# Two placements in an eight-core transformer layer: the softmax broadcasts one tile later, the last output block staggered

## The reference

```python
xn = layernorm(x)
q, k, v = split(xn @ w_qkv + b_qkv)            # 16 heads of 64
attn = softmax(q @ k.T * 64 ** -0.5)           # per head, 2048 x 2048
x = x + (attn @ v) @ w_proj + b_proj
h = fixed(layernorm(x) @ w1 + b1)              # 4096 wide, rounded to 1/256
h = fixed(piecewise_linear_gelu(h))
x = x + fixed(h @ w2 + b2)
```

## Time and profile before

| | us |
|---|---|
| median of 2 runs | 4026.95 (4025.5 to 4028.41) |
| profiled execution, slowest core 2 | 3910.7 span, 3912.19 device time |
| its two attention stages | 828.0 and 804.8 |
| ScalarE busy | 2506.1 (64%) |
| TensorE busy (matmuls) | 2639.1 (67%) |
| VectorE busy | 1966.8 (50%) |
| POOL busy | 665.8 (17%) |
| from issue to landing, store of `outt` / load of `x1rd2` | 2.1 / 4.2 |
| from issue to landing, DMA to `attn` | 1.9 |

### The profile page before, as it was taken

The page is one execution under the profiler, slowest core; times in us unless marked ns, Lnnn a source line. Parts: engine busy times, 40 slices in busy tenths (PEclk is TensorE's granted clock), DMA queues, the critical chain, the costliest instruction groups (busy, mean ns, idle before and its releaser), DMA issues.

```text
span 3910.7 us, 41130 instructions; the slowest of 8 cores (3899.2 to 3910.7 us)
## 1 busy us (share of the span) xinstructions
PE 2639.1 (67%) x10880; PEld 932.8 (24%) x10880; DVE 1966.8 (50%) x2865; ACT 2506.1 (64%) x3102; POOL 665.8 (17%) x1234
## 2 busy tenths in 40 slices
PE   0893757676778976777668244666767676667686
PEld 0441212111113411111111111222222222222232
DVE  3024434334440234343434257676767777676794
ACT  0314848485762185766758069787878777787893
POOL 1000000000010000000000233333333333342340
PEclk9997979898989998988989577787887887888898
DMA  8313010100013100001010654353444444353451
GB/s 183 79 22 103 26 55 30 41 14 25 24 18 72 22 3 21 28 4 45 3 45 4 125 86 65 61 85 55 80 72 70 69 76 69 70 77 70 68 92 50
DMA packets 206879, 215.91 MB, mean 55 GB/s; under 512 B 24000, under 2 KB 167360, under 8 KB 206656
## 3 DMA queue, kind: packets, MB, share of 16 engines
q0 software_dynamic: 169792, 95.82, 19.5%
q1 hardware_dynamic: 36864, 117.46, 9.3%
HBM read 265.90 MB, written 33.55 MB: 77 GB/s over the span
## 4 chain that ended last, share of the span: by engine, by line
PE 29%; ACT 19%; DVE 13%; DVEq 12%; ACTq 10%; issue 8%; DMA 7%; POOL 1%; SPq 0%; POOLq 0%
ACT PTb L646 11%; PE pAT L660 6%; PE pA L442 6%; DMA xstream<-x 5%; PE pA L633 5%; ACTq L1056 5%; ACTq L1021 4%; PE pBT L662 4%; DVEq L983 3%; PE pA L1089 3%; DVE fki L1036 3%; PE pA L479 3%; DVEq L1035 3%; DVE rbsb L530 2%; ACT fji L1025 2%
## 5 line engine op out<-in xcount | busy, mean ns | idle before, releaser
L646 ACT ACTIVATE PTb<-pA,negB 128x1024 bf16<-128x1024 f32 x1024 | 1104.4, 1112 | 474.1 <-PE pA L636 459.2
L956 PE MATMUL pA<-xn,w1s 128*128 128x512 bf16 x2048 | 615.2, 460 | 451.9 <-ACT ft L970 437.9
L819 POOL DMA_DIRECT2D w1s<-w x1024 | 554.9, 581 | 1039.5 <-PE pA L956 1014.1
L660 PE MATMUL pAT<-PTb,vtm 128*65 128x512 bf16 x1024 | 408.1, 399 | 270.0 <-ACT PTb L646 198.6
L1089 PE MATMUL pA<-w2b,gbuf 128*128 128x512 bf16 x2048 | 476.2, 393 | 91.7 <-ACT gbuf L1057 91.7
L633 PE MATMUL pA<-qfm,kfm 64*128 64x512 bf16 x1024 | 404.5, 404 | 48.6 <-DVEq L734 47.3
L956 PEld LDWEIGHTS pA<-xn,w1s 128*128 128x128 bf16 x2048 | 216.5, 111 | 817.3 <-issue 669.0
L662 PE MATMUL pBT<-PTb,vtm 128*65 128x512 bf16 x1024 | 406.2, 397 | 0.0
L636 PE MATMUL pA<-qfm,kfm 64*128 64x512 bf16 x1024 | 404.7, 405 | 0.0
L518 DVE COPY uAB<-pAT 65x512 f32<-65x512 f32 x64 | 43.9, 687 | 661.8 <-PE pBT L662 661.8
L602 POOL DMA_DIRECT2D attn<-stgB x64 | 33.6, 525 | 1735.9 <-PE pBT L662 1146.3
(11 more groups left out here) (79 smaller groups left out, 3143.9 us busy)
## 6 DMA issues: line engine op xcount, KB each, us to landing
w1s<-w POOLq DMA_DIRECT2D x1024, 64.0 KB, 2.5
xstream<-x SPq DMA_DIRECT2D x96, 512.0 KB, 3.9
x1rd<-x1s SPq DMA_DIRECT2D x64, 512.0 KB, 4.2
x1s<-x1t SPq DMA_DIRECT2D x32, 512.0 KB, 2.9
out<-outt SPq DMA_DIRECT2D x64, 256.0 KB, 2.1
wstr<-wqkv POOLq DMA_DIRECT2D x96, 128.0 KB, 5.4
w2b<-w POOLq DMA_DIRECT2D x32, 256.0 KB, 25.2
attn<-stgB POOLq DMA_DIRECT2D x64, 64.0 KB, 1.9
```

The costliest lines, as they stand in the source:

```text
L646: sc.activation(PT[:, kt % 2, :], pA[:, off:off + 1024], AF.Exp, bias=negB[:, 0:1], scale=SCALE).then_inc(c_s.sem, 1)
L660: t.matmul(pAT[0:65, :], lhs[:, 2 * pr, :], PT[:, kt % 2, 0:512], start=(kt == 0), stop=(kt == NKT - 1), skip_group_check=True)
L819: gp.dma_start(out=w1s[:, sl, dc, :], in_=w1[dc * 128:(dc + 1) * 128, grp * 256:(grp + 1) * 256]).then_inc(c_lw[sl].sem, 16)
L956: ins = t.matmul(pA[:, hb * 512:(hb + 1) * 512], w1s[:, sl, dc, (hm % 2) * 128:(hm % 2 + 1) * 128], xn2[:, bi % 2, dc, :], start=(dc == 0) ...
```

## The change

The four stages move one tile back in the pair loop, and the last block's evacuations are emitted one group behind their matmuls. For SP's queue the second edit means that the load of an even group is issued ahead of the store of the group before instead of behind it. No instruction is added or removed.

```diff
                     emit_pv(0)
-                    tmarks = {4: 0, 6: 1, 8: 2, 10: 3}
+                    tmarks = {5: 0, 7: 1, 9: 2, 11: 3}
                     for kt in range(2, NKT):
                         emit_st(kt, False)
                         if kt in tmarks and pending2[0] is not None:
...
                     g_done_of[(g - 3) // NHM] = c_s.n
-        for j in range(8):
+        w2_mm(NB - 1, 0)
+        for j in range(1, 8):
             w2_mm(NB - 1, j)
-            w2_ev(NB - 1, j)
+            w2_ev(NB - 1, j - 1)
+        w2_ev(NB - 1, 7)
         st_final = c_st.n
```

## The result

The changed kernel takes 0.987 of the time of the one before (95% interval 0.982 to 0.991). Executions with one die or both at a lower granted clock take up to 110 us longer, and the two behind the starting median of 4026.95 lie with those; without that the kernel before takes 3914 to 3926 us as a rule, most often near 3918, and the changed one 3873 to 3882, most often near 3880. That is 37 to 39 us less. The profiled executions took 3912.19 and 3881.47 us: 0.992, or 31 us, and 3912.19 is the shortest time of the kernel before on record. The forecast was 19 us, from a starting point of 4027 that was wrong.

What follows compares the result with a forecast made beforehand. Neither ScalarE nor TensorE bounds attention alone; they hand work to and fro, two tiles per 2.27 us. Savings of 17.5 us in 42 pairs and 1.7 in the first blocks, together 19, off 4026.95 give 4008 us, range 3994 to 4024.

Steps and rivals of the forecast that it cites:

- The wait and the slot: Pair loop: first broadcast at tile 5 avoids the reciprocal wait (0.29 us) and TensorE's short slot (0.19) per waiting pair.
- Rival A: Pair loop: only the wait goes, 0.29 us a pair; 11 us saved, 4016 us; chance 0.17.
- rival B: Pair loop: nothing that can be told, the exponential's delay being absorbed elsewhere; 4022 to 4027 us; chance 0.12.
- The low pairs: Pairs starting with TensorE at its lower clock: 20.47 us before, 0.1 us saved by the edit, so 20.37 after.
- The last block: End of the last stage: three later loads issued ahead of output stores; saves 0 us, at most 1 us.
- What else moved: Pair loop: second multiply and its DMA go 1.1 us later, covered by the long period; costs 0 us.
- The base: Starting time: saved microseconds taken off the runs' median of 4026.95 us, 116 us above the profiled span of 3910.7.
- The count of low starts: Six later query blocks: pairs starting at TensorE's lower clock go from 21 to 16 of 42; 17.5 us saved there altogether.
- rival D: Pair starts: nearly no starts at TensorE's lower clock, 4 of 42; 32 us saved in all, 3995 us; chance 0.10.
- Outside the 42 pairs: First two query blocks: 9 full-clock pairs with broadcasts save 0.19 us each by the slot, 1.7 us together.

Runs made afterwards that it cites:

- e3: The changed kernel with its stages at tiles 6, 8, 10, 12 instead of 5, 7, 9, 11: full-clock pair 18.35 us, period 19.51 us.
- e4: The changed kernel with its stages at tiles 7, 9, 11, 13 instead of 5, 7, 9, 11: full-clock pair 18.15 us, period 19.31 us.
- e6: The changed kernel with both broadcast matmuls left out inside the pair loop: full-clock pair 18.15 us, period 19.31 us.
- e2: The kernel before with only the last block's edit, stages left at tiles 4, 6, 8, 10: ratio 1.0015 (0.997 to 1.006).
- e7: The changed kernel with the third stage, the second broadcast, at tile 10 instead of 9: full-clock pair 18.35 us, 108 low starts of 336.
- v1: The lagged kernel: the changed kernel with three exponential buffers, not two, and value matmuls one tile later; 0.9585 of the kernel before, 3749 to 3775 us.

## Why the prediction was right, and where it failed

**The wait and the slot: right.** "With the long slot, a waiting pair should save 0.29 + 0.19 = 0.48 us: 19.80 becomes 19.32." It is 19.31, and e3, e4 and e6 measured the terms apart: 0.30 for the wait, 0.19 for the slot, 0 for what is left. Waits are 8, 42.2 us. Rival A, which had 18.35 for a pair, is excluded by the changed kernel's 18.15, rival B by the six blocks' sum. The low pairs' 20.37 is their median period, 20.37. One reading beside it was wrong without touching the sum: in the kernel before only the broadcast at tile 4 falls into a short slot. It turns the alternation round, and the one at tile 8 already stands in a long slot, 0.75 us (in the pair of the earlier trace rows from scores at 1665.53 to value matmuls at 1666.28). The whole 0.48 lies at tile 4: the spacing behind it is 1.50 us before and 1.01 in the changed kernel, as medians. The Trainium skill (TensorE: Matmul & The Clock Gate, Part 2, Back-to-back issue gap) has about 0.216 us from one 512-column matmul to the next at the full clock. The broadcasts here don't agree: from scores to broadcast it is 0.32 us again in the changed kernel.

**The last block: right.** 0 us; e2's ratio is 1.0015.

**What else moved: right in kind.** The later multiply and DMA cost nothing; e4, two tiles later still, has the same 18.15.

**The base: wrong, and the largest error.** "The saved microseconds are taken over as they are: 4008", added to 4026.95. The execution that every term came from took 3912.19 us, and those like it, 3914 to 3926. The 116 us weren't time that lies around the span. The profile's own span and time were 1.5 us apart, and that was in front of me; the sum should have stood on 3912 and would have given 3893, with a range of 3879 to 3909. The 3880 measured would have lain in that by one microsecond. On the usual 3918 the same savings give 3899, with a range of 3885 to 3915, and 3880 lies outside that too: the range allowed 3 to 33 us to be saved, and 37 to 39 were. So of the 128 us between forecast and time some 109 are the base, and the rest is the saving, forecast at half its size.

**The count of low starts: the size was off.** "I take 16 of 42": core 0 has 10, core 2 has 4, the mean of the eight cores is 5. That is rival D, which had 0.10, at the cores' mean (n = 4 there, 30 us in the six blocks). On the slowest core 32 x 19.32 + 10 x 20.37 = 821.9 by the forecast's own terms; measured, with the ends of pairs added, 817.40 + 6.96 = 824.4, bumps of about 3 us included. This term was too small by 7 us on the slowest core. The step that failed is the sentence that a new period shuffles the starts: it treated the count as luck and the edit as neutral to it. e7 and the counts by last spacing show that the edit acts on it, through the parity of the slots. The very reading that forecast the 0.19 had the cause in it: turning the alternation round also changes which spacing comes last.

By the Trainium skill (the same page, Part 1) the activity monitor runs free of the kernel; the 2 to 10 low starts on the eight cores of one execution agree with that. The effect of a pair's last spacing stands in the counts above.

**Outside the 42 pairs: too small.** The forecast had 1.7 us in the first two blocks and nothing elsewhere. The first two blocks gave 5.1 (4.3 in the mean of the cores, with about one low start fewer on each), the stretches between blocks 8.6 (2.6 in the mean). What the latter are isn't shown.

## What to carry to other kernels

When two engines hand tiles to and fro over two buffers, write down each tile's start and look whether the spacing alternates: an operation inserted every so many tiles is free in one slot and costs in the next (as long as the slots are there: in v1 it costs again), and the profile's row of waits (5 us here) shows neither the slot's cost nor the delay that the wait leads to (0.29 us each). Before choosing a slot, ask whether the producer's next piece of work needs to stand behind the consumer of the last at all; one more buffer was worth three to four times as much. And take the base of a forecast from the execution that its terms were read from.

## What the runs showed of the hardware

Exponentials of 128 x 1024 last 1.11 us each in the record but follow each other every 1.00 us when nothing holds them up: their ends overlap the next start. A bound of 16 x 1.11 = 17.8 us for a pair would have hidden most of the lagged kernel's gain; it took 16.30.

TensorE's clock fell to 1.2 GHz at the start of a pair or not, and that went with whether 0.25 us of idle time stood one tile earlier or later: 2% after the one, 31 to 52% after the others, with busy time per pair the same (9.5 us). A pair that starts at 1.2 GHz takes 1.06 us more in the changed kernel (20.37 against 19.31) and 0.70 in the one before.
